# Row scales of two layernorms applied behind their products, a new order on every engine and constant products in TensorE's waits, in a two-image vision tower

## What is computed

```python
x = einsum('bchpwq,dcpq->bhwd', patches, conv_w) + conv_b         # 2 x 256 x 128
for l in range(2):
    y = ln(x, ln1_g[l], ln1_b[l])
    q, k, v = split(y @ qkv_w[l])                                  # 8 heads of 64
    q = softmax(q, axis=-1) * scale                                # over a head's columns
    k = softmax(k, axis=-2)                                        # over the tokens
    x = x + (q @ (k.T @ v)) @ out_w[l] + out_b[l]
    x = x + gelu(ln(x, ln2_g[l], ln2_b[l]) @ ff1_w[l] + ff1_b[l]) @ ff2_w[l] + ff2_b[l]
h = ln(x, lnf_g, lnf_b) @ head_w + head_b                          # 2 x 256 x 192
q, k, v = split(layernorm(h) @ W_qkv)                              # 12 heads of 16
q, k = elu(q) + 1, elu(k) + 1
h = h + ((q @ (k.T @ v)) / (q @ sum(k))) @ W_out + b_out
h = h + new_gelu(layernorm(h) @ (w_fc * C0).T + b0) @ (w_proj * C1).T + b1
```

## Time and profile before

| | kernel before |
|---|---|
| median of three runs | 136.7 us (136.61 to 137.17) |
| profiled execution | 136.95 us, span on the core 135.2 us |
| mean granted TensorE clock | 0.987 |
| instructions in the span | 2174 |

### The profile page before, as it was taken

The page is one execution under the profiler, slowest core; times in us unless marked ns, Lnnn a source line. Parts: engine busy times, 40 slices in busy tenths (PEclk is TensorE's granted clock), DMA queues, the critical chain, the costliest instruction groups (busy, mean ns, idle before and its releaser), DMA issues.

```text
span 135.2 us, 2174 instructions
## 1 busy us (share of the span) xinstructions
PE 119.6 (88%) x818; PEld 104.0 (77%) x818; DVE 77.6 (57%) x241; ACT 61.9 (46%) x147; POOL 48.7 (36%) x60
## 2 busy tenths in 40 slices
PE   6859999899999998985999999479987789999992
PEld 6759999686986996863699588368676677998991
DVE  6000064998898258199899834726667687246102
ACT  3000131698953852397467269114551344391420
POOL 0000011245642983865350694334022018951000
PEclk9999999999999999999999999977999999999999
DMA  4999989995000000000000000000000000000101
GB/s 124 367 402 410 423 293 411 413 387 224 7 2 0 0 5 0 0 0 0 0 0 5 0 0 0 2 2 0 0 5 0 0 0 0 5 0 0 58 0 58
DMA packets 3884, 12.18 MB, mean 90 GB/s; under 512 B 441, under 2 KB 1817, under 8 KB 3618
## 3 DMA queue, kind: packets, MB, share of 16 engines
q1 hardware_dynamic: 3874, 12.05, 23.3%
HBM read 11.65 MB, written 0.39 MB: 89 GB/s over the span
## 4 chain that ended last, share of the span: by engine, by line
PE 53%; DVE 25%; ACT 8%; DMA 6%; POOL 3%; issue 3%; SPq 1%
PE bank L318 9%; DMA embed_sb<-in_embed 6%; PE bank L494 5%; PE bank L412 4%; PE bank L374 3%; PE bank L400 3%; POOL rstd L1756 3%; DVE xn L942 3%; PE bank L327 2%; PE bank L351 2%; PE bank L430 2%; DVE nkmax L959 2%; DVE q L971 2%; DVE stats L923 2%; DVE y L938 2%
## 5 line engine op out<-in xcount | busy, mean ns | idle before, releaser
L1756 POOL TENSOR_TENSOR rstd<-mv,minus_half 128x2 f32<-128x2 f32 x14 | 10.1, 721 | 45.6 <-DVE mv L929 45.6
L1774 POOL TENSOR_TENSOR qn<-q,rqsum 128x512 f32<-128x512 f32 x8 | 8.4, 1044 | 13.4 <-DVE rqsum L979 13.4
L318 PE MATMUL bank<-embed_sb 128*128 128x128 f32 x64 | 8.4, 283 | 2.0 <-DMA embed_sb<-in_embed 2.0
L318 PEld LDWEIGHTS bank<-embed_sb 128*128 128x128 f32 x64 | 7.9, 198 | 2.5 <-DMA embed_sb<-in_embed 2.4
L923 DVE BATCH_NORM_STATS2 stats<-bank 128x6 f32<-128x128 f32 x4 | 1.1, 288 | 14.7 <-PE bank L323 14.7
L1522 ACT ACTIVATE hid<-bank,small_sb 128x256 f32<-128x256 f32 x16 | 6.7, 473 | 5.7 <-PE bank L407 5.6
L412 PE MATMUL bank<-restw,hid 128*128 128x128 f32 x64 | 8.8, 281 | 0.3 <-ACT hid L1522 0.2
L494 PE MATMUL bank<-projw,patches_sb 128*128 128x192 f32 x48 | 8.9, 328 | 0.0
L393 PE MATMUL bank<-cw,qT 128*128 128x128 f32 x64 | 8.8, 279 | 0.0
L412 PEld LDWEIGHTS bank<-restw,hid 128*128 128x128 f32 x64 | 7.9, 192 | 0.9 <-ACT hid L1522 0.5
L1500 ACT ACTIVATE qkw_hi<-qkvw 128x512 fp32r<-128x512 f32 x4 | 2.5, 627 | 13.2 <-DMA qkvw<-in_qkv_w 13.2
(11 more groups left out here) (161 smaller groups left out, 344.8 us busy)
## 6 DMA issues: line engine op xcount, KB each, us to landing
embed_sb<-in_embed SPq DMA_DIRECT2D x3, 768.0 KB, 7.7
patches_sb<-in_patches SPq DMA_DIRECT2D x2, 1024.0 KB, 11.7
restw<-in_rest_w SPq DMA_DIRECT2D x2, 768.0 KB, 14.8
qkvw<-in_qkv_w SPq DMA_DIRECT2D x3, 256.0 KB, 10.9
qkvw<-in_qkv_w SPq DMA_DIRECT2D x1, 768.0 KB, 15.7
fcw<-in_fc_w SPq DMA_DIRECT2D x1, 768.0 KB, 17.1
embed_sb<-in_embed SPq DMA_DIRECT2D x1, 576.0 KB, 3.9
aqkvw<-in_aqkv_w SPq DMA_DIRECT2D x1, 576.0 KB, 14.8
```

The source lines that it names most:

```text
L318: mm = nc.tensor.matmul(CONV_BANK[i][t][:, 0:D], left, embed_sb[:, c, 0:D], start=(c == 0), stop=False)
L1756: return nc.gpsimd.tensor_tensor(rstd[i][:], mv[i][:, :, 1], minus_half[:], ALU.pow)
L1774: return nc.gpsimd.tensor_tensor(qn[:, t, :].rearrange("p (h d) -> p h d", h=HEADS), q[:, t, :].rearrange("p (h d) -> p h d", h=HEADS), rq ...
```

## The change

The computed values are the same; these things change.

- **Row scales behind the products.** For the final norm and the third one (ahead of the head and of the attention block of the tail) VectorE writes xn = x - mean (`centre`) without rstd. ScalarE applies the final norm's gain (`gain`); its offset goes through `headw` once (`widen_offset`, `head_offset`, `head_row_ready`), and `head_rows` becomes product*rstd + head_row. The third norm's rstd goes into the scale of `phi3_exp`, of a new ScalarE step `phi3_plus_one` and of `v3_to_sbuf`, now one step per tile. `phi3_min` vanishes; `phi3_max` takes max(min(e, 1), p) from two SBUF tiles. Waits for normalised tiles become waits for centred ones (`centred_last`, `centred3`).
- **Order.** All five lists are written in a new order. The loads of image 0's weights and norm rows come ahead of the second half of image 1's patches. In layer 0, image 0's norm, keys and queries stand ahead of most of image 1's patch products, and the masks' products stand there too. In layer 1 image 0 comes first, then image 1. In the tail Q3's turn stands ahead of context3, and fc3 and proj3 are interleaved otherwise. On ScalarE the two splitting copies of `fcw` stand together between the second layer's affine step of image 0 and its first gelu. On GpSimd bias rows, low parts and mixing move, several of them directly behind a power. PSUM banks are given out anew.
- **Constant products.** `warm_up` stands at six places among TensorE's waits, eight products in all: ahead of ff1 of image 1 in layer 0 (two), behind turn3 of image 0 (two), behind v3_rows of image 0, ahead of attend3 of image 0, behind Q3's turn of image 1, and ahead of fc3 of image 0.

The diff, cut to its core:

```diff
             load_embed(0, 1, "embed0")
             load_embed(1, 4, "embed1")
+            load_embed(4, 8, "embed2")
+            load(convb_sb[:], convb, "cb")
             load_embed(8, 12, "embed3")
             load_embed(12, 16, "embed4")
-            load_embed(4, 8, "embed2")
-            load(convb_sb[:], convb, "cb")
             load_patches(0, 8, "patches1a")
+            load(norm_rows_sb[0][:], norm_rows0.to_broadcast([P, GROW]), "rg")
             load(qkvw[0][:, INNER:2 * INNER], qkv_w[0][:, INNER:2 * INNER], "qkv0k")
+            load(small_sb[:], small, "small")
             load(qkvw[0][:, 0:INNER], qkv_w[0][:, 0:INNER], "qkv0q")
+            load(headw[:], head_w, "head")
+            load(aqkvw[:], aqkv_w, "aqkv")
             load_patches(8, 16, "patches1b")
-            load(norm_rows_sb[0][:], norm_rows0.to_broadcast([P, GROW]), "rg")
-            load(aoutw[:], aout_w, "aout")
-            load(small_sb[:], small, "small")
             load(norm_rows_sb[1][:], norm_rows1.to_broadcast([P, GROW]), "rows")
             load(rows_sb[:], rows.to_broadcast([P, NROW]), "rows")
-            load(aqkvw[:], aqkv_w, "aqkv")
+            load(mix_sb[:], mix, "mix")
+            load(qkvw[0][:, 2 * INNER:], qkv_w[0][:, 2 * INNER:], "v0")
+            load(aoutw[:], aout_w, "aout")
             load(restw[1][:], rest_w[1], "rest1")
-            load(headw[:], head_w, "head")
-            load(qkvw[0][:, 2 * INNER:], qkv_w[0][:, 2 * INNER:], "v0")
             load(qkvw[1][:], qkv_w[1], "qkv1")
-            load(restw[0][:], rest_w[0], "rest0")
-            load(mix_sb[:], mix, "mix")
             load(projw[:], proj_w, "proj")
             load(fcw[:], fc_w, "fc")
+            load(restw[0][:], rest_w[0], "rest0")
...
+            def head_offset():
+
+                return nc.tensor.matmul(HROW_BANK[:, 0:E], lnf_b_wide, headw[:], start=True, stop=True)
...
             conv(1, 4, 6)
-            conv_bias(0, 1).then_inc(conv_done, 1)
+            pe.wait_ge(y_ready, 2)
+            pe.wait_ge(loaded["small"], 16)
+            turn(TURN1_BANK[0], y[0]).then_inc(y_turned, 1)
             conv(1, 6, 8)
+            pe.wait_ge(y_high, 1)
...
+            pe.wait_ge(x_new, 2)
+            warm_up(bank[0], 2)
             ff1_high(1, 0)
-            k_high(2, 1)
...
+            pe.wait_ge(loaded["head"], 16)
+            head_offset()
...
+            pe.wait_ge(centred_last, 2)
+            turn(TURNF_BANK[0], xn[0]).then_inc(last_turned, 1)
             ff1_low(3, 2).then_inc(ff1_done, 1)
             ff1_high(3, 3)
-            pe.wait_ge(gelu_ready, 13)
-            ff2(3, 0).then_inc(ff2_done, 1)
...
+            pe.wait_ge(centred3, 2)
             turn3(TURN3_BANK[0], TURN3_REST_BANK[0], xn[0]).then_inc(turned3, 1)
-            ff2(3, 3).then_inc(ff2_done, 1)
+            pe.wait_ge(x_new, 7)
+            warm_up(bank[5], 2)
             pe.wait_ge(high3, 1)
             qk3_high(0, 0)
...
+            warm_up(bank[6], 1)
             pe.wait_ge(phi3_ready, 2)
-            pe.wait_ge(v3_ready, 1)
+            turn_heads(Q3_BANK[0], qk3[0]).then_inc(q3_turned, 1)
...
+            warm_up(bank[2], 1)
             pe.wait_ge(attention3_columns, 1)
             pe.wait_ge(loaded["aout"], 16)
...
+            turn_heads(Q3_BANK[1], qk3[1]).then_inc(q3_turned, 1)
+            warm_up(bank[6], 1)
+            pe.wait_ge(v3_ready, 4)
             context3(1).then_inc(context3_done, 1)
...
+            warm_up(bank[3], 1)
             fc3(0, 0).then_inc(fc3_done, 1)
...
+            def centre(i, t, src, width):
+                return nc.vector.tensor_scalar(xn[i][:, t, 0:width], src[i][:, t, 0:width], mv[i][:, t, 0:1], None,
+                                               ALU.subtract)
+
+            def widen_offset():
+                return nc.vector.tensor_scalar(lnf_b_wide, ones[:, 0:P], col("lnf_b"), None, ALU.mult)
+
+            def head_row_ready():
+                return nc.vector.tensor_tensor(head_row[:], HROW_BANK[:, 0:E], bias_row("head_b", 0, E), ALU.add)
...
             def head_rows(i, t):
-                return nc.vector.tensor_tensor(h[i][:, t, :], HEAD_BANK[i][:, t * E:(t + 1) * E],
-                                               bias_row("head_b", 0, E), ALU.add)
+                return nc.vector.scalar_tensor_tensor(out=h[i][:, t, :], in0=HEAD_BANK[i][:, t * E:(t + 1) * E],
+                                                      scalar=rstd[i][:, t:t + 1], in1=head_row[:], op0=ALU.mult,
+                                                      op1=ALU.add)
...
-            def phi3_min(i, t):
-
-                return nc.vector.tensor_scalar(qk3m[i][:, t, :], qk3e[i][:, t, :], 1.0, None, ALU.min)
-
             def phi3_max(i, t):
 
-                return nc.vector.scalar_tensor_tensor(out=qk3[i][:, t, :], in0=QK3_BANK[i][t][:, 0:2 * E], scalar=1.0,
-                                                      in1=qk3m[i][:, t, :], op0=ALU.add, op1=ALU.max)
+                return nc.vector.scalar_tensor_tensor(out=qk3[i][:, t, :], in0=qk3e[i][:, t, :], scalar=1.0,
+                                                      in1=qk3p[i][:, t, :], op0=ALU.min, op1=ALU.max)
 
...
+            def gain(i, bankof):
+                return nc.scalar.activation(yT[i][:], bankof[:, 0:TOKENS], ACT.Copy, scale=col("lnf_g"))
...
             def phi3_exp(i, t):
-                return nc.scalar.activation(qk3e[i][:, t, :], QK3_BANK[i][t][:, 0:2 * E], ACT.Exp)
-
-            def v3_to_sbuf(i):
-                return nc.scalar.activation(v3[i][:].rearrange("p t c e -> p (t c) e")[:, :, 0:EC],
-                                            V3_BANK[i][:, 0:TILES * E].rearrange("p (n e) -> p n e", e=EC), ACT.Copy)
+                return nc.scalar.activation(qk3e[i][:, t, :], QK3_BANK[i][t][:, 0:2 * E], ACT.Exp,
+                                            scale=rstd[i][:, t:t + 1])
+
+            def phi3_plus_one(i, t):
+                return nc.scalar.activation(qk3p[i][:, t, :], QK3_BANK[i][t][:, 0:2 * E], ACT.Identity,
+                                            bias=ones[:, 0:1], scale=rstd[i][:, t:t + 1])
+
+            def v3_to_sbuf(i, t):
+                return nc.scalar.activation(v3[i][:, t, :, 0:EC],
+                                            V3_BANK[i][:, t * E:(t + 1) * E].rearrange("p (n e) -> p n e", e=EC),
+                                            ACT.Copy, scale=rstd[i][:, t:t + 1])
...
+            act.wait_ge(ff_in_high, 3)
+            affine(0, TURN2_BANK[2], col("ln2_g", 1), col("ln2_b", 1)).then_inc(ff_in_ready, 1)
+            evict(fcw_parts[0][:, 0, :], fcw[:, 0, :])
+            evict(fcw_parts[0][:, 1, :], fcw[:, 1, :])
             act.wait_ge(ff1_done, 10)
             gelu(2, 0).then_inc(gelu_ready, 1)
...
             pool.wait_ge(mean2_ready, 2)
             inverse_deviation(0).then_inc(deviation2_ready, 1)
+            add_row(0, bias_row("ff2_b", 0)).then_inc(x_and_ff2_bias, 1)
+            low_part(ff1w_parts[0][1][:], ff1w(0), ff1w_parts[0][0][:]).then_inc(ff1_weight_low, 1)
...
             inverse_deviation(1).then_inc(deviation1_ready, 1)
-            mix_fc(1).then_inc(fc_mixed, 1)
+            mix_fc(1)
+            pool.wait_ge(loaded["proj"], 16)
+            mix_proj()
...
             pool.wait_ge(mean4_ready, 4)
             inverse_deviation(1).then_inc(deviation4_ready, 1)
+            add_row3(0, projb[:]).then_inc(h_and_proj_bias, 1)
+            add_row3(1, projb[:]).then_inc(h_and_proj_bias, 1)
```

1059 lines of the change are left out of this document (524 added, 535 removed).

## The result

| | before | after |
|---|---|---|
| median, 20 executions each, same chip | 137.83 us | 135.50 us |
| ratio of the two, 95% interval | | 0.986, 0.983 to 0.989 |
| profiled execution | 136.95 us | 136.73 us |
| its span | 135.2 us | 134.9 us |
| TensorE busy, share of the span | 119.6 us, 88% | 122.9 us, 91% |

The change makes the kernel 1.4% faster. 132.4 us, or 3.1%, had been predicted. One thing must be known to read the times: executions of the same kernel differ in TensorE's mean granted clock, and a ratio leaves out those more than 1.5% above the fastest of their kernel, while a median takes all. Of after's twenty, eleven ran at 1.0 (median 135.31 us) and nine at 0.987 (median 136.73 us). The profiled one is of the second kind. The kernel before ran at 0.973 to 0.987 in all 39 executions that stood beside the experiments, never at 1.0.

A forecast was written before the change was run, and what follows sets the result against it. TensorE, busy 88%, bounds the kernel, with slack around the last feed-forward and in the tail. 136.95 - 2.0 + 3.2 - 3.5 - 2.7 + 0.7 = 132.65 us, as a median 132.4 us (3.1% faster); range 129.0 to 136.0 us.

The forecast's parts named there:

- The last feed-forward: Image 0's add to turn3, layer 1: scale behind the product saves 3.5 us; bounds 1.8 (clock falls again) and 4.3 us.
- Caught steps: GpSimd work queued behind rstd delays VectorE's SBUF steps at three places: 3.2 us lost, bounds 0 and 5.2 us.
- the second place: Layer 1, first norm of image 1: mix_fc(1) and mix_proj pieces catch xg and y steps, 1.0 us added.
- the first place: Layer 0, second norm of image 0: add_row and the low part of ff1w delay the normalise steps, 1.4 us.
- VectorE gets in nowhere: Slower rival: queued GpSimd steps hold VectorE until the queue is empty, and the clock falls twice; 138.4 us, chance 0.08.
- The row at 88.43 us: Profile row before the change, a GpSimd step just begun when a caught normalise ended: VectorE gets in between queued GpSimd steps.
- The clock: Rival: the clock falls again around layer 1, 1.7 us each time; 134.1 us once, 135.8 us twice; chance 0.20.
- the two places named: Where the clock might fall: TensorE nearly idle 2.5 us ahead of turn(y[1]), and about half idle around ff2 of layer 1.
- The order of the first 85 us: Start to 85.5 us: the new order fills idle time, net gain 2.0 us, bounds 0 and 3.4 us.
- the walk: New TensorE order traced with old rows' durations: fills 3.4 of 3.8 us idle, one fcw-copy stall costs 1.4 us.
- The tail: 96 to 125 us: fewer powers, no phi3_min and Q3's turn earlier save 2.7 of 3.3 us TensorE idle time.
- Constant products: Eight added products take 2.6 us of TensorE, 0.7 us on the path: 0.45 ahead of ff1, the rest in the tail.

The follow-up runs named there:

- the wait on GpSimd: The changed kernel, with mix_fc(1) and mix_proj on GpSimd waiting until both y steps of image 1 in layer 1 are written: 133.78 us, ratio 0.971.
- the kernel before with one wait: Kernel before, with mix_fc(1) on GpSimd waiting for both y steps of image 1 in layer 1: median 137.14 us, ratio 0.983 from two executions, unsettled.
- the kernel with scales and waits: Kernel before plus row scales alone; on GpSimd mix_fc(1) waits for y and the low part of fcw for the fourth norm: 134.97 us, ratio 0.980.
- its three waits: The changed kernel, with GpSimd waiting for VectorE's y or normalise steps at all three places of caught steps: 132.55 us, ratio 0.962.

## Why the prediction was right in places and missed the time

**The last feed-forward: right in size, for partly other reasons.** Predicted -3.5 us, measured -3.60 us. The scales alone gave 1.9 us in the old order at full clock, and 0.7 us where the clock fell again, below the lower bound of 1.8 us that the step gave for that case. The remaining 1.7 us came only with the new order, in which turn(xn) doesn't stand behind ff1's wait for yT, nor turn3 behind ff2. The step had put them down to the caught normalise, the slow head and the slow ff2; these went, but in the old order their going gave little, since the turn of xn then waits for ff1 and turn3 for ff2. That the sum agrees to a tenth is in part luck.

**Caught steps: right in place, too large in size.** Predicted 1.4 + 1.0 + 0.8 = 3.2 us; measured 0.55 + 1.67 + 0.6 = 2.8 us. But the 1.0 us counted only what the change adds at the second place, where the kernel before had a catch already. That one cost 1.0 us, so the change added 0.7 us there, and 0.55 + 0.7 + 0.6 = 1.8 us in all. At the first place most of the second catch is there (1.59 us instead of 0.57 us for the pair), but of that 1.02 us only 0.55 us reached the path. At the second place xg was held for 1.49 - 0.34 = 1.15 us and the two y for 1.10 - 0.61 = 0.49 us. VectorE did get in between pieces there, so "VectorE gets in nowhere" did not happen in after. It did happen in the row scales on the kernel before, where one step was held past three whole GpSimd steps. The row at 88.43 us, on which the rival's 0.08 rested, shows that VectorE can get in, not that it always does. The page "SBUF — State Buffer" of the Trainium skill (Who interferes with whom) has the loser wait for the other's instruction. The y steps between the pieces agree with that; the 5.52 us pair is longer than any single instruction it ran beside, so the runs show that the wait can outlast one. phi3_max, with two SBUF inputs, never ran beside GpSimd in after and kept 0.54 to 0.56 us.

**The clock: the rival came true in part.** In the profiled execution it fell at the first of the two places named, and cost 1.40 us (the rival said 1.7 us); nine of twenty executions have that one's mean clock. The forecast plus one fall is 134.1 us; after's median is 135.5 us, so this alone does not explain the miss. The Trainium skill, "TensorE: Matmul & The Clock Gate" (Part 4, PE-mode transpose), says that a transpose doesn't count as busy in the same way. Here the turns stand behind the wait (62.84 us and on), with products ahead of it up to 61.0 us. With the wait on GpSimd the same turns stand there with 0.17 us of idle ahead of y's, and the clock stays at 1.0 in five of six executions. So without the idle time the fall became rare; turns and idle time weren't varied apart. Nor does the idle time decide by itself: eleven executions of after kept the clock, presumably behind the same wait (none of them was profiled), and in the kernel before with one wait it fell at 54 us behind rows that are the same in the kernel before, which kept it. What tips it is open.

**The order of the first 85 us: the first step that failed.** Predicted a gain of 2.0 us. This is not the middle between 0 and 3.4 us, as the step says, but 3.4 - 1.4 us: all the idle time that the walk filled, less the one stall that it saw. With no catch and no low clock, the add still comes at 85.30 us against 85.54 us before: 0.24 us, and 0.7 us with the pair of constant products (0.45 us) counted apart. Even that is owed to the catch in the kernel before, which the forecast had left where it was: without this 1.0 us the order brings 0.7 - 1.0 = -0.3 us. Profiled executions differ by some 0.5 us in when their loads arrive (the first turn of image 1 stands at 26.18 us before, at 26.67 us in the kernel with scales and waits), so the new order is about even with the old one, and the 2.0 us are not there. The walk was too kind: idle time of 3.8 us in before's stretch was counted as slack, and the waits that came with the new order were not seen. With no step caught, TensorE still waits 1.14 us for the first y (at 17.79 us), 0.58 us ahead of the pair of constants and 0.98 us for the gelu ahead of ff2. The stall by the fcw copies that was seen (1.4 us) measured 1.1 us.

**The tail: the second step that failed.** Predicted -2.7 us; without the catch it brought 40.24 - 39.6 = 0.6 us. TensorE's idle time before, 3.27 us, was taken as work that could be packed, and the two powers and phi3_min as links whose going shortens the path. But its largest waits before stand in the attention block, and none of them ends with a power:

```profile
103.57 1.11 PE L474 MATMUL bank<-kv,patches_sb 96*128 96x102 f32 x8 [0.78 <-ACT patches_sb L1500]
...
105.95 0.64 PE L467 MATMUL bank<-small_sb,embed_sb 128*96 128x128 f32 x4 [0.69 <-DVE embed_sb L1053]
...
111.55 0.91 PE L458 MATMUL bank<-v,embed_sb 128*96 128x102 f32 x8 [0.67 <-DVE embed_sb L1025]
```

With the scales in the old order and no normalise pair caught, the stretch from turn3 to the end of the last product takes 130.13 - 92.53 = 37.60 us, against 37.59 us before: the scales alone shorten it by nothing. The 0.6 us came with the new order. Without constant products the idle time is still 2.45 us, spread over several waits of 0.2 to 0.6 us each. Which link is the last to bind was not settled; fc3's place was worth 0.15 to 0.3 us.

**Constant products:** predicted 0.7 us, measured 0.4 us for the pair and at most 0.3 us for the six.

The sum with measured terms, from before's profiled 136.95 us: order +0.3, pair +0.45, catches +1.8, clock +1.4, middle -3.6, tail -0.6 make 136.7 us, and the profiled execution took 136.73 us. It has to close, since the terms are read from the same traces; what it shows is where the miss lies. Against the forecast's 132.65 us the order is off by 2.3 us, the tail by 2.7 - 0.25 - 0.6 = 1.85 us and the clock by 1.4 us; catches (1.4 us) and middle (0.1 us) go the other way. An execution at full clock lacks the 1.4 us.

The best steady kernel of these runs is after with its three waits, the fcw copies moved, the pair of constants out and fc3's two products moved back: 130.79 us, 4.8% faster than before, with a spread of 130.69 to 131.01 us.

## What to carry to other kernels

When GpSimd's next instruction follows a power that VectorE also waits for, make it wait for VectorE's steps: three such lines took the kernel after from a ratio of 0.986 to 0.962. Take such a catch out of the kernel before, too, before crediting a new order with what it brings. Idle time of an engine that waits for a chain is not slack; a gain there must be argued link by link, and filling it with constant products only hides it in the busy column. A row scale moved behind its product is worth the power only where the path waits for that power (nothing in the tail here), and beyond that whatever collision it avoids or, by coming earlier, runs into.

## What the runs showed of the hardware

A VectorE step that reads and writes SBUF alone (xn, 0.3 us) can be held past several GpSimd steps in a row, 5 us in one case, and elsewhere gets in between two of them; reductions from PSUM beside the same queue kept their 0.68 us, and two centre steps beside a power of 128x2 elements kept 0.47 us. TensorE's granted clock can go either way in executions of one and the same kernel: nine of after's twenty have a mean of 0.987, and the one profiled lost 1.40 us behind a wait of 1.82 us for y, while the other eleven ran at 2.4 GHz throughout. Two kernels with the same instructions and the same idle time up to 54 us part there: one falls to 1.2 GHz, the other stays at 2.4 GHz. A saving of under 2 us can move later work into a collision that costs more, as the row scales on the kernel before suggest with 143 against 136 to 139 us.
